# Routing shares carried in the scattered rows, and gathers that add into the residual rows, in a two-layer transformer with 16 experts

## What is computed

```
h = concat(conv_patches(x) + pos, txt)                 # [16, 113, 192]
h = h + attention0(layernorm(h))
u = layernorm(h)
t = u * rsqrt(mean(u*u) + eps) * scale
vals, idx = top_k(t @ gate_w.T + gate_b, 4)            # 4 of 16 experts
w = softmax(vals)                                      # the 4 shares
y_e = (silu-like gate(t @ w1[e] + b1[e])) @ w2[e] + b2[e]
h = h + u + sum over the 4 experts of w_e * y_e
h = h + attention1(layernorm(h))                       # 8 heads and 2 chained groups
h = h + ffn1(layernorm(h))                             # router, 12 heads, MLP 768
```

## Time and profile before

| | us |
|---|---|
| three timed runs, median (lowest, highest) | 975.55 (973.28, 978.21) |
| the profiled execution, its own time | 979.58 |
| its span, first to last instruction | 977.8 |
| busy: PE / PEld | 797.9 (82%) / 572.6 (59%) |
| busy: DVE / ACT / POOL | 495.4 (51%) / 306.4 (31%) / 365.4 (37%) |
| mean granted TensorE clock | 0.855 |

### The profile page before, as it was taken

How to read it: one execution, slowest core, us unless ns; L and a number is a source line. 1 busy time by engine, 2 the same in 40 slices (tenths; PEclk the granted TensorE clock), 3 DMA queues, 4 the chain that set the end, 5 groups by cost and what they waited for, 6 DMA issues and landing times.

```text
span 977.8 us, 14811 instructions
## 1 busy us (share of the span) xinstructions
PE 797.9 (82%) x4860; PEld 572.6 (59%) x4860; DVE 495.4 (51%) x1223; ACT 306.4 (31%) x571; POOL 365.4 (37%) x233
## 2 busy tenths in 40 slices
PE   7988872279999999988979788779799799888572
PEld 4665662147667777756767574554656656656351
DVE  4354655524644444658676965363824743634210
ACT  1121321023333333333424337144352252342200
POOL 3015888786820287758786100010200100000000
PEclk9787765569999999997979899858789879989795
DMA  8831113334543344444111000000000000000000
GB/s 235 238 106 46 35 29 72 68 79 115 119 124 88 87 117 114 103 127 98 35 29 31 1 1 1 1 1 1 2 0 1 14 0 0 13 3 1 15 0 15
DMA packets 81395, 52.96 MB, mean 54 GB/s; under 512 B 42942, under 2 KB 76719, under 8 KB 80305
## 3 DMA queue, kind: packets, MB, share of 16 engines
q1 hardware_dynamic: 27330, 29.82, 10.9%
q0 software_dynamic: 40960, 11.98, 6.8%
q10 hardware_dynamic: 13040, 10.30, 3.7%
HBM read 29.53 MB, written 21.69 MB: 52 GB/s over the span
## 4 chain that ended last, share of the span: by engine, by line
PE 60%; POOL 16%; DVE 9%; issue 6%; ACT 3%; DMA 3%; SPq 0%; DVEq 0%; ACTq 0%; POOLq 0%
POOL work L223 8%; POOL xs_scratch L212 6%; PE ex_up L1143 6%; PE ex_up L1144 6%; PE ps L2270 4%; PE ps L2201 3%; PE ex_yp L1166 3%; PE ex_yp L1167 3%; PE ps L1355 2%; PE ps L1357 2%; PE ps L1350 2%; PE ps L2210 2%; PE ps L1356 2%; PE a_ps L392 1%; PE ps L1366 1%
## 5 line engine op out<-in xcount | busy, mean ns | idle before, releaser
L223 POOL DMA_INDIRECT work<-ys_scratch,place x64 | 153.8, 2403 | 87.5 <-DMA ys_scratch<-ex_yb 57.5
L212 POOL DMA_INDIRECT xs_scratch<-e_t,e_routed x64 | 152.8, 2387 | 43.0 <-issue 29.3
L1242 DVE TENSOR_SCALAR ex_bb<-ex_up 128x384 f32<-128x384 f32 x44 | 24.5, 558 | 118.6 <-PE ex_up L1144 87.7
L1143 PE MATMUL ex_up<-e_wa,ex_x 128*128 x176 | 75.1, 509 | 8.4 <-issue 6.9
L1144 PE MATMUL ex_up<-e_wb,e_ex_x 65*128 x176 | 73.9, 501 | 0.0
L2480 POOL TENSOR_TENSOR H<-H,f_hh 113x768 f32 (+1 forms) x4 | 7.2, 1810 | 146.7 <-DVE f_hh L2623 146.7
L2458 POOL TENSOR_SCALAR f_veps<-f_mv 113x4 f32<-113x4 f32 x10 | 1.9, 194 | 144.8 <-DVE f_mv L2520 144.8
L1201 ACT ACTIVATE ex_sg<-ex_up 128x384 f32<-128x384 f32 x44 | 21.6, 492 | 106.3 <-PE ex_up L1144 96.9
L2406 ACT ACTIVATE f_pT<-ps 113x452 f32<-113x452 f32 x48 | 26.2, 546 | 77.5 <-PE ps L2210 77.4
L1144 PEld LDWEIGHTS ex_up<-e_wb,e_ex_x 65*128 65x128 f32 x176 | 34.4, 196 | 24.7 <-issue 2.1
L2201 PE MATMUL ps<-f_k,f_q 32*113 32x113 f32 x384 | 32.5, 320 | 16.9 <-DVE f_p L2560 15.8
(11 more groups left out here) (372 smaller groups left out, 1921.9 us busy)
## 6 DMA issues: line engine op xcount, KB each, us to landing
ex_xb<-xs_scratch SPq DMA_DIRECT2D x88, 96.0 KB
ys_scratch<-ex_yb ACTq DMA_DIRECT2D x44, 192.0 KB
xs_scratch<-e_zeros SPq DMA_DIRECT2D x62, 96.0 KB
e_wa<-in_wa SPq DMA_DIRECT2D x4, 1152.0 KB
e_wb<-in_wb SPq DMA_DIRECT2D x4, 576.0 KB
e_wa<-in_patches SPq DMA_DIRECT2D x4, 432.0 KB, 9.3
out<-H SPq DMA_DIRECT2D x4, 339.0 KB
w4a<-in_w4a SPq DMA_DIRECT2D x1, 1216.0 KB
```

Of the source, the lines that this page charges most:

```text
L212: nc.gpsimd.indirect_dma_start(out=dram.xs, out_offset=bass.IndirectOffsetOnAxis(ap=S.pos[:, j, k:k + 1], axis=0), in_=S.t[:, j, :], in_of ...
L223: nc.gpsimd.indirect_dma_start(out=S.yk[:, it % 2, j, k, :], out_offset=None, in_=dram.ys[it // X.steps], in_offset=bass.IndirectOffsetOnA ...
L1143: mm(o, x1[:, p % 3, t], S.wa[:, bass.ds(w, 2 * I)], start=True, stop=False)
```

## The change

1. The scratch row grows from 192 to 208 floats. `weights` spreads the four shares over the 16 experts with two more DVE instructions (113x256) and writes them beside the token's features in `S.t`, so that they travel with each scattered row. The zero tile and the ring `xb` grow alike.
2. A scatter now waits for its step's shares too. For that, in step 1 `top_exp(0)` and `weights(0)` stand before `positions(0)` (ACT: right behind `later_loads`, which issues two DMAs).
3. The table gets one more row, `sat`: the column in which a block's share stands. ACT's new `share_copy(p)` loads that number into a register for each of the pair's blocks and copies one column of `xb` into a small tile. The place in `xb` is free for SP's next load only when this copy is done too.
4. `y_copy` is two instructions for a pair, each scaled by its block's share.
5. The gathers add straight into `H` (`compute_op=ALU.add`). They go choice by choice over the four sequences, and each waits until the gather before it into the same sequence has landed, that is the fourth before it.
6. `mixed` (64 DVE instructions) is gone, and so is the buffer `yk`. The wait for the gathers stands before `h_stat`, at n = 2 in attention 1 and at the last pair but two in the experts.

```
 class X:
     rows = 128
+    row = D + E
...
+READY = 3
...
         nv.tensor_copy(S.wat[:, at], T.ew[:]).then_inc(S.table_ok, 1)
+        nv.tensor_scalar(S.sat[:, at], T.eb[:], float(E - 1), float(D), ALU.min, ALU.add).then_inc(S.table_ok, 1)
...
 def collected(nc, pool, dram, S, it, c0, c1):
-    if it >= 2:
-        pool.wait_ge(S.mixed, G * TOPK * (it - 1))
     for c in range(c0, c1):
-        j, k = c // TOPK, c % TOPK
+        k, j = c // G, c % G
+        if it or k:
+            pool.wait_ge(S.got[j], 16 * (TOPK * it + k))
         nc.gpsimd.indirect_dma_start(
-            out=S.yk[:, it % 2, j, k, :], out_offset=None, in_=dram.ys[it // X.steps],
-            in_offset=bass.IndirectOffsetOnAxis(ap=S.place[:, it * G + j, k:k + 1], axis=0)).then_inc(S.got[it], 16)
-def mixed(nc, dve, S, it, k):
...
+            out=S.H[0:N, it * G + j, :], out_offset=None, in_=dram.ys[it // X.steps],
+            in_offset=bass.IndirectOffsetOnAxis(ap=S.place[:, it * G + j, k:k + 1], axis=0), compute_op=ALU.add
+            ).then_inc(S.got[j], 16)
+def collected_ok(eng, S, it):
     for j in range(G):
+        eng.wait_ge(S.got[j], 16 * TOPK * (it + 1))
...
             def scatter(it, c0, c1):
                 pool.wait_ge(*done(picked, it, POS))
+                pool.wait_ge(*done(shared_out, it, GATES))
...
             def weights(it):
...
+                nv.tensor_tensor(w4[:], e4[:], bc(r4[:].unsqueeze(2), [N, G, TOPK]), ALU.mult).then_inc(shared_out.sem, 1)
+                dve.wait_ge(*done(shared_out, it, SHARE))
+                nv.tensor_tensor(spread[:], oh(it), bc(w4[:].unsqueeze(2), [N, G, E, TOPK]), ALU.mult).then_inc(shared_out.sem, 1)
+                dve.wait_ge(*done(shared_out, it, SPREAD))
+                nv.tensor_reduce(S.t[:, it * G:(it + 1) * G, D:X.row], spread[:], AX.X, ALU.add).then_inc(shared_out.sem, 1)
...
                 if b >= RING:
                     sp.wait_ge(xt_ps, (b - RING) // 2 + 1)
+                    sp.wait_ge(share_ok, b - RING + 1)
...
+            def share_copy(p):
+                if p >= 4:
+                    act.wait_ge(y_ok, 2 * (p - 3))
+                for h in range(2):
+                    b = 2 * p + h
+                    at = act.value_load(S.sat[0:1, b:b + 1], min_val=D, max_val=X.row - 1)
+                    cp(share[:, p % 4, h:h + 1], xb[:, b % RING, bass.ds(at, 1)], ACT.Copy).then_inc(share_ok, 1)
...
-                s = (2 * p) % RING
-                cp(yb[:, s:s + 2, :], yp[:, 0:2 * D].rearrange("p (h d) -> p h d", h=2), ACT.Copy).then_inc(y_ok, 1)
+                act.wait_ge(share_ok, 2 * (p + 1))
+                for h in range(2):
+                    cp(yb[:, (2 * p + h) % RING, :], yp[:, h * D:(h + 1) * D], ACT.Copy, scale=share[:, p % 4, h:h + 1]).then_inc(y_ok, 1)
...
                     x_copy(p + 2)
+                    share_copy(p + 2)
...
-                if NPAIR - 7 <= p < NPAIR - 7 + TOPK:
-                    mixed(nc, dve, S, 0, p - (NPAIR - 7))
                 if p == NPAIR - 3:
-                    dve.wait_ge(S.mixed, G * TOPK)
+                    collected_ok(dve, S, 0)
                     h_stat(nc, dve, S, 0)
...
-                    if n in (0, 1) and not last:
-                        mixed(nc, dve, S, it + 1, 2 * n)
-                        mixed(nc, dve, S, it + 1, 2 * n + 1)
                     if n == 2 and not last:
-                        dve.wait_ge(S.mixed, G * TOPK * (it + 2))
+                        collected_ok(dve, S, it + 1)
                         h_stat(nc, dve, S, it + 1)
```

More of the change, by code:

```diff
@@ L343, in attn0_phase @@
         TOP, E4, IDX, IDXF, OH, MASK, CARRY, OHS, POSF, POS, PICKS = 0, 4, 5, 9, 10, 11, 12, 16, 17, 18, 19
-        S4, R4, SHARE = range(3)
-        picked, e4x_ok, shared_out = sem("picked", PICKS), sem("e4x_ok", 1), sem("shared_out", 3)
+        S4, R4, SHARE, SPREAD, GATES = range(5)
+        picked, e4x_ok, shared_out = sem("picked", PICKS), sem("e4x_ok", 1), sem("shared_out", 5)
         KT = CHANNELS * PATCH * PATCH // 128
@@ L670, in body @@
                 o_copy(it)
-                if not first:
+                if it > 1:
                     top_exp(it - 1)
@@ L1062, in sem @@
             return ctx.enter_context(nc.semaphore("ex_" + name))
-        xb, yb = sb("xb", [R, RING, D]), sb("yb", [R, RING, D])
+        xb, yb = sb("xb", [R, RING, X.row]), sb("yb", [R, RING, D])
+        share = sb("share", [R, 4, 2])
         x1, x2 = sb("x1", [LO, 3, 2 * R]), S.ex_x2
@@ L1076, in experts_phase @@
         x_in, y_out = [sem(f"x_in{i}") for i in range(RING)], [sem(f"y_out{i}") for i in range(PAIRS)]
[L1077 to L1078 removed]
+        xt_ps, x1_ok, x2_ok, up_ps, sg_ok, bb_ok, gl_ok, ac_ok, at_ps, a1_ok, a2_ok, y_ps, y_ok, place, share_ok = (sem(n) for n in (
+            "xt_ps", "x1_ok", "x2_ok", "up_ps", "sg_ok", "bb_ok", "gl_ok", "ac_ok", "at_ps", "a1_ok", "a2_ok", "y_ps", "y_ok", "place", "share_ok"))
         S.y_out, S.y_ps, S.y_turns, S.y_last = y_out, y_ps, NPAIR, NPAIR
@@ L1215, in store @@
                               ).then_inc(y_out[p % PAIRS], 16)
+            act.wait_ge(S.table_ok, READY)
             x_copy(0)
+            share_copy(0)
             x_copy(1)
+            share_copy(1)
             sigmoid(0)
@@ L2749, in program @@
         S.a0_o2, S.a0_tS2 = sb("a0_o2", [HI + 1, G, N]), sb("a0_tS2", [HI + 33, G, N])
-        S.place, S.w4 = sb("place", [N, B, TOPK], U32), sb("shares", [N, B, TOPK])
-        S.count_ok, S.shift_ok, S.place_ok, S.tails_ok, S.table_ok, S.zeroed, S.experts_in, S.mixed, S.shifted, S.count_ps, S.table = (ctx.enter_context(nc.semaphore(n)) for n in (
-            "count_ok", "shift_ok", "place_ok", "tails_ok", "table_ok", "zeroed", "experts_in", "mixed", "shifted", "count_ps", "table"))
+        S.place = sb("place", [N, B, TOPK], U32)
+        S.count_ok, S.shift_ok, S.place_ok, S.tails_ok, S.table_ok, S.zeroed, S.experts_in, S.shifted, S.count_ps, S.table = (ctx.enter_context(nc.semaphore(n)) for n in (
+            "count_ok", "shift_ok", "place_ok", "tails_ok", "table_ok", "zeroed", "experts_in", "shifted", "count_ps", "table"))
         S.sent, S.got = ([ctx.enter_context(nc.semaphore(f"{n}{i}")) for i in range(STEPS)] for n in ("sent", "got"))
@@ L2762, in program @@
         S.a1_v, S.a1_out1 = sb("a1_v", [N, G, 8, 32]), sb("a1_out1", [D // 2 + 1, GN])
-        S.work = sb("work", [128, 2 * G * TOPK * D])
-        S.yk = S.work[0:N, :].rearrange("p (r g k d) -> p r g k d", r=2, g=G, k=TOPK)
+        S.work = sb("work", [128, 4320])
         with ExitStack() as early:
@@ L2771, in program @@
             S.wat, S.rat = eb("wat", [1, X.halves * X.blocks], I32), eb("rat", [1, X.halves * X.blocks], I32)
+            S.sat = eb("sat", [1, X.halves * X.blocks], I32)
             S.ex_x2, S.ex_a2 = eb("ex_x2", [HI + 1, 3, 2 * X.rows]), eb("ex_a2", [HI + 1, 2, 2 * X.rows])
-            S.tat, S.zeros = eb("tat", [1, X.halves, E], I32), eb("zeros", [X.rows, D])
-            S.t = eb("t", [N, B, D])
+            S.tat, S.zeros = eb("tat", [1, X.halves, E], I32), eb("zeros", [X.rows, X.row])
+            S.t = eb("t", [N, B, X.row])
             T = S.tb = Names()
@@ L2893 @@
     dram.fc2b = give("fc2b", f["fc2_b"][None])
-    dram.xs = nc.dram_tensor("xs_scratch", [X.halves * X.half, D], F32, kind="Internal").ap()
+    dram.xs = nc.dram_tensor("xs_scratch", [X.halves * X.half, X.row], F32, kind="Internal").ap()
     dram.ys = [nc.dram_tensor(f"ys{h}_scratch", [X.blocks * X.rows, D], F32, kind="Internal").ap() for h in range(X.halves)]
```

22 lines of the change are left out of this document (8 added, 14 removed).

## The result

The changed kernel takes 1090.73 us as the median of 4 runs (1073.71 to 1095.17), the kernel before 975.55: ratio 1.1105, 95% interval 1.1008 to 1.1202. The forecast was 971.8 us, the range 966 to 1008. Rival (a), an adding gather that is dearer to issue, is what happened. The profiled execution took 1095.17 with a span of 1093.4, against 979.58 and 977.8. It and one other of the four are slow executions, at a granted clock of 0.812 and 0.820 against 0.822 and 0.832, so the ratio goes by the other two, 1088.31 and 1073.71.

The account below looks back on a forecast made before the run. Bounds: POOL's scatters, then PE in the experts, then POOL's gathers up to h_root(2). Gathers' issue -1.5 and mixing gone -2.8 made -4.3 from 975.55, 971.3; half a microsecond for waits and loads gave 971.8, range 966 to 1008.

Parts of the forecast that it names:

- Rival (a): POOL's gathers before h_root(2): an adding gather is dearer to issue; 990 to 1094 us by its extra price; chance 0.27.
- Gathers, issue: POOL's gathers: 1.5 us less without mixing beside them; adding gather taken at the plain 2.36 us, far end 4.73.
- d: Extra issue time of each adding gather on POOL, in us; 0.18 eats the gain, 2.36 is a doubling.
- 56d - 10: Loss in us from dearer adding gathers on POOL over both halves, d more on each, when that is more.
- Shares before the scatters: Step 0's start: first scatter 1.2 us later, swallowed by POOL's 1.41 idle before the root; cost 0, at most 1.
- Longer rows: Scatters on POOL: 832-byte rows go in as many pieces as 768, issue unchanged; cost 0, range 0 to +5 us.
- Experts: Experts' stretch: ACT's added 2.0 to 2.1 us a pair just fits its 2.12 idle; cost 0, other end 44 us.
- The new wait: Gathers: each waits for the fourth before it, 9.1 to 9.8 us against 10.68; hidden with 0.9 to 1.6 to spare.
- rival (b): Gathers: an adding one lands over 9.8 us after its start, some 4x for excess x; 2 gives 980; chance 0.10.
- Mixing gone: Attention 1, step 2: DVE loses 5.45 us of mixing, PE and ACT follow in part; -2.8 us, range to -5.4.
- Rival (c): DVE's relief comes through whole, 5.4 us in step 2 and a microsecond more in steps 0 and 1; 968; chance 0.10.
- (d): Experts: ACT's added work outgrows its idle; 0.3 us a pair is 13 us, giving 985; chance 0.05.

Follow-up runs that it names:

- e4: Changed kernel with other gathers by step: 384-byte rows, 64 rows adding, 64 rows plain; one run, issue 4.33, 1.41 and 0.92 us.
- e8: Changed kernel with its adding gathers at 128 rows in place of 113, scatters unchanged; 984.50 us, 1.0113.
- e3: Kernel before with the changed kernel's adding gathers and chained waits, no mixing, shares computed but not used; 1079.74 us, 1.1102.
- e1: Changed kernel with only the addition left out of its gathers, which overwrite the residual rows; 981.74 us, 1.0054.
- v128: Kernel before with scatters and gathers of 128 rows in place of 113; 940.01 us, 0.9588.
- e9: Kernel before with plain gathers of 127, 116, 114 and 100 rows by step; one run, issue 2.55, 1.26, 1.13 and 1.01 us.
- after128: Changed kernel with scatters and gathers of 128 rows in place of 113; 937.43 us, 0.9621.
- v128b: v128 run again, beside after128; 945.34 us, 0.9722.
- e2: Changed kernel's shares path with the kernel before's plain gathers, VectorE adding the buffers, one buffer for clamped values; 989.72 us, 1.0188.
- e7: e2 with each share copied from a fixed column, without ScalarE's register loads, so wrong shares scale the results; 984.20 us, 1.0056.
- e5: Kernel before with plain gathers of 128, 112, 120 and 96 rows by step, scatters of 113; one run, 970.28 us.
- e6: Changed kernel with adding gathers of 112, 96, 104 and 80 rows by step; one run, issue 1.50, 1.45, 1.60 and 1.43 us.

## Why the prediction was wrong, by its own steps

**The step that failed** is "Gathers, issue": "What an adding gather costs to issue no row shows ... I take 2.36, the nearest row". It is 4.33, d = 1.97, 83% of the way to the far end of 4.73. The choice between the ends was the error: equal prices of plain scatter and plain gather say nothing of a gather that adds. The Trainium skill's sentence on two read descriptors ("Collectives: The Full Stack", bandwidth ceiling), which it says of the reduce step of a collective, pointed to the right rival. It wasn't a fixed doubling: e4 and e8 give 1.41 against 0.92 at 64 rows and 1.54 against 0.95 at 128. The range then stopped at 1008, though the far end's own sum was 1094.

The place that rival (a) named was right, its formula roughly. 56d - 10 counts the 56 gathers before `h_root(2)` and gives 100.3; the trace shows 90.9 there (e3: 92.5). It had kept the gaps at every sixteenth indirect DMA, and between adding gathers they are gone: idle of 3.98, 1.91 and 3.88 us before a gather became 0.30, and only one of 1.94 is left, a chained wait. Why they are gone no run shows. What it left out are the last eight gathers, which hold `h_root(3)` 10.0 us longer, and the 8.9 and 5.7 us before and behind. That its 1094 for a doubled price stands so near the measured 1090.73 is luck: with the measured d it gives 971.8 + 100.3 = 1072.

A row in hand said more than I took from it. The earlier trace rows gives 292 bytes a packet to rows of 768. I read that as "goes in pieces" and went on to bytes. With e1 the packets of one DMA can be counted: its 45056 less the 320 of each plain gather leave 384 a scatter, and the changed kernel's 141312 less those leave 1824 an adding gather. 1824 is 16 x 114, 320 is 16 x 20, and for 128 rows they are 144 (e8: 33792 - 24576, over 64), 16 x 9, and 48 (v128), 16 x 3. In e9, stretches with gathers of one count only give 96 each for 116 rows (384 for four), 80 for 114 (640 for eight) and 48 for 100 (384 for eight), multiples of 16 too. So 113 rows read like sixteen shares of 113 short pieces and one more packet each; plain, several pieces share a packet; adding, each is a packet of its own. The pieces themselves were not seen, this is how the counts fit.

**Shares before the scatters**: right. First scatter at 82.70 (expected 83.2), the root after the five at 96.13 with no idle (96.7).

**Longer rows**: cost right, reason not. The scatter stays at 2.38 us, though its packets went from 320 to 384.

**Experts**: ACT fits, as worked out. In an undisturbed pair the period is 4.79 us and ACT still idles 1.36 us before its sigmoid. Yet the stretch from first to last y_copy is 240.9 us, before 207.3, well over the 3 us that I had allowed. ACT's added instructions alone don't do it: e8 has the same and takes 209.8. Two parts make up the 33.6 us. From the first y_copy to the first gather are 123.9 us, before 113.5, and no adding gather has run yet. In e1 and e8, whose order of work is the same up to there, they are 117.6 and 116.4, in e3, without shares, 115.3. So a few of these ten belong to the shares' path, whose cost the sum put at 0, and the rest to this one execution. From the 28th sigmoid at 351.58 to the 44th at 452.06, as the adding gathers run, a pair takes 6.28 us (100.5 over 16), 24 us more. Adding gathers without shares lengthen the whole to 219.7 (e3), shares without them to 215.4 (e2). Both together come to more than the sum, in the one trace there is of the changed kernel. The first part reached the end, as the 8.9 us by which the first gather is late. The second did not, since POOL's own order from 343 to 656 was longer.

**The new wait**: hidden, as forecast, by other numbers, but for one. An adding gather lands 14.5 us after its start in the median (13.5 to 21.3), far over the 9.8 of rival (b). But the fourth before it now started 18.5 us earlier. Only where a landing took longer than that did a wait show, 1.94 us before the gather at 485.08 (3.74 in e3). The chain of waits of the changed kernel:

```profile
474.10 15.17 DMA H<-ys_scratch,place
...
640.67 14.12 DMA H<-ys_scratch,place
```

The second is the last gather's: it lands at 654.79, h_stat begins at 654.91 and the last root at 656.56. Against 8.22 in the earlier trace rows its 14.12 is 5.9 of the 10.0 us between `h_root(2)` and `h_root(3)`.

**Mixing gone**, -2.8: could not show behind POOL. In after128 against v128 and v128b it and the shares' path cancel within what the runs can tell. Rival (c) could not show either, (d) did not occur in undisturbed pairs.

**What stays open**: which part of the shares' path costs its half to two per cent (e2, e7), and by what way GpSimd's DMAs of 113 rows slow the experts. That they do is shown by e8 and v128, which change the row count: the stretch of y_copies is 209.8 us against 240.9, and 201.7 against 207.3. PE's issue waits at the up-projection are 20.0 us in the changed kernel, 5.7 in e8, 6.9 before and none in v128. Register loads go the same way: on ACT 0.58 us in the median and up to 2.20, in e8 0.29; those of PE's weight columns 0.63 against 0.31 (e3, without shares: 0.64). That PE's issue waits are these loads is likely, and not shown.

```profile
L1210 ACTq TENSOR_LOAD <-e_sat x88: 271/583/2204, 194.6 to 448.0; - x88
```

```profile
L1212 ACTq TENSOR_LOAD <-e_sat x88: 271/286/1497, 193.9 to 417.1; - x88
```

The first line is of the changed kernel, the second of e8.

## What to carry to other kernels

Before an operation moves from an engine that has time for it into a transfer, ask which engine prepares that transfer and whether it stands on the path: here 21.9 us of VectorE's adds were traded for 123.3 us more of issue on the one engine whose order sets the end. Where no row prices the new form and it stands on the path, let the range reach the dear end, however near a plain row may be. And look at the row count first: 15 useless rows more made every indirect DMA of this kernel 2.5 times cheaper to issue. That gained 36 us of 976, more than the best case that I had thought the change capable of (968).

## What the runs showed of the hardware

Issue time of one indirect DMA on GpSimd, all with rows of 768 bytes. "Rows on each" is the row count over its largest divisor up to 16. The times are those of most gathers of a count: 127, 116, 114 and 100 rows from e9, plain 128, 120, 112 and 96 from e5, adding 112, 104, 96 and 80 from e6, 64 from e4, adding 128 from e8, 113 from e1 and the changed kernel:

| rows | largest divisor up to 16 | rows on each | plain us | adding us |
|---|---|---|---|---|
| 127 | 1 | 127 | 2.55 | |
| 113 | 1 | 113 | 2.38 | 4.33 |
| 116 | 4 | 29 | 1.26 | |
| 114 | 6 | 19 | 1.13 | |
| 100 | 10 | 10 | 1.01 | |
| 104 | 13 | 8 | | 1.60 |
| 120 | 15 | 8 | 0.98 | |
| 128 | 16 | 8 | 0.95 | 1.54 |
| 112 | 16 | 7 | 0.94 | 1.50 |
| 96 | 16 | 6 | 0.92 | 1.45 |
| 80 | 16 | 5 | | 1.43 |
| 64 | 16 | 4 | 0.92 | 1.41 |

Plain it is 0.84 us and 0.0136 for each row in the third column, adding 1.33 and 0.0264 (from 8 and 113 rows; the others fit within 0.06). For the adding gather no count between 8 and 113 on each was run. Adding gathers of 113 rows of 384 bytes cost the same as of 768 (e4). The Trainium skill, "DMA: Bandwidth & Descriptors", section "Why a DMA increments its semaphore by 16 and not by 1", has the division: a DMA goes to the largest number of engines up to 16 that divides its slowest dimension. The issue times go by that divisor at all twelve counts. That a prime count goes to one engine does not agree with the traces: 113 rows are 1824 packets, not 113 and a few, and from 545 to 600 us, where a gather starts every 4.62 us and lands after 14.1, so that about three are under way, POOL's queue takes 32.9% of the time of 16 engines, 5.3 of them:

```profile
q0 software_dynamic: 21327, 1.19, 32.9%
```

The landing follows the row count too: 2.6 us in the median for 128 rows in v128, 8.22 for one gather of 113; adding, 3.6 in e8 against 14.5.
